# Weighted sums of an adjacency network: narrow matmuls, one row at a time, in place of 512-column blocks and a mask

## The reference

```python
hi = jnp.einsum('bsh,hk->bsk', x, W1[:H])
hj = jnp.einsum('bsh,hk->bsk', x, W1[H:])
h = jax.nn.relu(hi[:, :, None, :] + hj[:, None, :, :] + b1)
y = jnp.einsum('bijk,kl->bijl', h, W2) + b2
y = _layernorm(y, gamma, beta)
out = jnp.einsum('bij,bijh->bih', adj, y)      # the weighted sums
...
x = _layernorm(x + first_layer(x, adj), axis=-1)
x = _layernorm(x + attention_layer(x, adj), axis=-1)
```

## Time and profile before

| | |
|---|---|
| median of 3 runs | 2533.56 us (2532.02 to 2536.31) |
| the profiled execution | 2531.95 us |
| its span, first to last instruction | 2529.9 us |
| TensorE matmuls busy | 2416.6 us (96%) |
| ScalarE busy | 2233.7 us (88%) |
| VectorE busy | 2121.4 us (84%) |
| GpSimd busy | 2024.9 us (80%) |
| TensorE's mean granted clock | 0.986 |

### The profile page before, as it was taken

One profiled execution on the slowest core, in us unless ns is written; L12 is line 12 of the kernel. 1 busy time (PEld: TensorE's weight loads), 2 busy tenths in 40 slices (PEclk: granted clock), 3 DMA queues, 4 the chain that ended last, 5 costly groups with the idle time before them and its releaser, 6 DMA issues.

```text
span 2529.9 us, 182178 instructions
## 1 busy us (share of the span) xinstructions
PE 2416.6 (96%) x73792; PEld 2115.5 (84%) x73792; DVE 2121.4 (84%) x17817; ACT 2233.7 (88%) x3841; POOL 2024.9 (80%) x1227
## 2 busy tenths in 40 slices
PE   8999999999999999999999999999999999999997
PEld 7888888888888888888888888888888888888885
DVE  7888888888888888888888888888888888888887
ACT  7998898888988989888898898988889888898896
POOL 8888887887887878878788787887888877888784
PEclk9999999999999999999999999999999999999999
DMA  0000000000000000000000000000000000000000
GB/s 22 11 10 15 15 10 15 10 15 15 10 15 10 16 15 10 15 11 14 15 10 15 12 14 15 10 16 15 10 15 10 15 15 10 16 14 11 15 8 12
DMA packets 48663, 33.51 MB, mean 13 GB/s; under 512 B 6208, under 2 KB 47808, under 8 KB 47808
## 3 DMA queue, kind: packets, MB, share of 16 engines
q1 hardware_dynamic: 46512, 21.12, 3.0%
q10 hardware_dynamic: 1296, 0.20, 0.0%
HBM read 17.11 MB, written 4.19 MB: 8 GB/s over the span
## 4 chain that ended last, share of the span: by engine, by line
PE 81%; ACT 9%; issue 6%; DVE 4%; POOL 0%; ACTq 0%; DMA 0%; DVEq 0%
PE y_ps L529 60%; PE agg_ps L574 16%; ACT h L288 4%; ACT y L270 3%; DVE squares L515 3%; PE prep_ps L529 2%; PE tail_ps L529 1%; ACT beta_part L328 1%; DVE q L515 1%; PE att_ps L529 1%; ACT ln_v L317 0%; POOL h L259 0%; ACTq L367 0%; DMA beta_rows<-in_L_gnn_beta_dram 0%; ACT rstd L322 0%
## 5 line engine op out<-in xcount | busy, mean ns | idle before, releaser
L259 POOL TENSOR_TENSOR h<-bT,aT 128x1024 f32<-128x1024 f32 x1024 | 1952.7, 1918 | 449.7 <-PE y_ps L529 429.4
L529 PEld LDWEIGHTS y_ps<-w_pair,h 128*32 128x32 f32 x65536 | 1897.4, 111 | 320.0 <-issue 205.5
L529 PE MATMUL y_ps<-w_pair,h 128*32 128x128 f32 x65536 | 2021.6, 275 | 92.4 <-issue 65.5
L515 DVE CUSTOM_DVE_ANT_0 squares<-y_ps,y 128x128 bf16<-128x128 f32 x8192 | 1849.6, 286 | 290.4 <-ACT y L270 283.4
L270 ACT ACTIVATE y<-y_ps 128x508 f32<-128x508 f32 x2048 | 1165.4, 596 | 257.3 <-PE y_ps L529 254.7
L288 ACT ACTIVATE h<-h 128x1024 f32<-128x1024 f32 x1024 | 1084.0, 1059 | 9.5 <-POOL h L259 9.5
L515 DVE DVE_READ_ACCUMULATOR2_ANT q<- 128x1 f32 x8192 | 680.2, 83 | 0.0
L574 PE MATMUL agg_ps<-y,wz 128*32 128x512 f32 x4096 | 568.5, 592 | 0.0
L574 PEld LDWEIGHTS agg_ps<-y,wz 128*32 128x32 f32 x4096 | 158.2, 110 | 2.8 <-issue 2.4
L433 DVE TENSOR_SCALAR tail_ps<-q,bnorm 128x128 f32<-128x128 f32 x64 | 22.7, 354 | 55.9 <-issue 54.5
L451 DVE SCALAR_TENSOR_TENSOR o_sb<-agg_ps,part,o_sb 128x128 f32<-128x128 f32 x192 | 66.6, 347 | 0.2
(11 more groups left out here) (90 smaller groups left out, 734.2 us busy)
## 6 DMA issues: line engine op xcount, KB each, us to landing
x_in<-in_x_dram SPq DMA_DIRECT2D x64, 64.0 KB, 2.3
adj_in<-in_adj_dram SPq DMA_DIRECT2D x64, 64.0 KB, 2.6
x_res<-in_x_dram SPq DMA_DIRECT2D x64, 64.0 KB, 2.1
adj_res<-in_adj_dram SPq DMA_DIRECT2D x64, 64.0 KB, 2.7
out_dram<-x_out SPq DMA_DIRECT2D x64, 64.0 KB, 2.2
w<-in_L_gnn_W_dram ACTq DMA_DIRECT2D x1, 64.0 KB, 2.3
w1a<-in_L_gnn_W_dram SPq DMA_DIRECT2D x1, 64.0 KB, 2.3
w1b<-in_L_gnn_W_dram SPq DMA_DIRECT2D x1, 64.0 KB, 2.3
```

The costliest lines, as they stand in the source:

```text
L259: nc.gpsimd.tensor_tensor(h[:, u % HRING].rearrange("k (r g) s -> k r g s", g=GROUPS), bT[:, p, :].unsqueeze(1).unsqueeze(1).broadcast_to( ...
L515: last = nc.vector.tensor_tensor_reduce(out=squares[:, k % YRING, n, :], in0=y_ps[k % YRING][:, n, :], in1=y[:, p, i, :], scale=1.0, scala ...
L529: last = nc.tensor.matmul(dst[cols], lhsT[:, cols], rhs, start=True, stop=True, tile_position=(0, g * GROUP))
```

## The change

One matmul now handles one row of each group: `wz` has for each group and each of 32 rows a 32-column block with one column that is not zero, and the matmul streams 128 columns. All 32 rows of a group accumulate in the same 128 columns of `agg_ps`, so that partition 32g+r ends with the sum of its own row. The masks, `part` and the semaphores for them are gone; VectorE copies the 128 columns once, at (u, e) = (0, 1). The number of columns that are streamed per slot is the same, the number of matmuls is four times as large. The order on TensorE changes too: the rows stand one or two at a time behind each of the banks k = 8 to 31, in place of 4 rows behind a unit. GpSimd writes `wz` with another pattern of the same number of elements; `wz` has four times the size.

```diff
@@ -54,10 +54,9 @@
 
 
 
-    CHUNK = 4
-    CHUNKS = GROUP // CHUNK
     POOL_WEIGHTS_UNIT, POOL_RESIDUAL_UNIT = 5, 6
-    SUM_AT = {u: c for c, u in enumerate((4, 6, 7, 9, 10, 12, 13, 15))}
+    SUMS_FROM = 8
+    SUMS_STEP = QUARTS - SUMS_FROM
 
     ctx = ExitStack()
     with ctx:
@@ -106,8 +105,7 @@
         q = sb("q", [S, 2, S])
         ln_v = sb("ln_v", [S, S])
         rstd = sb("rstd", [S, S])
-        wz = sb("wz", [S, GROUPS, CHUNKS, GROUP])
-        part = sb("part", [S, CHUNK])
+        wz = sb("wz", [S, GROUPS, GROUP, GROUP])
         o_sb, oT_sb = sb("o_sb", [S, K]), sb("oT_sb", [K, S])
         x1e = sb("x1e", [S, K + 1])
         st1, mv1, ln1, rs1 = sb("st1", [S, 6]), sb("mv1", [S, 2]), sb("ln1", [S, 1]), sb("rs1", [S, 1])
@@ -220,7 +218,7 @@
                 pool.wait_ge(adjT_sb_s, t)
                 if early >= 2:
 
-                    pool.wait_ge(agg_done, (t - 1) * CHUNKS)
+                    pool.wait_ge(agg_done, t - 1)
                 else:
                     pool.wait_ge(s_zero, 1)
                 if early >= 3:
@@ -229,9 +227,9 @@
 
                 flat = wz[:]
                 columns = bass.AP(flat.tensor, flat.offset,
-                                  [list(flat.ap[0]), [CHUNKS * GROUP, GROUPS], [GROUP + CHUNK, CHUNKS], [1, CHUNK]])
-                nc.gpsimd.tensor_tensor(columns, adjT[:, 1 - p, :].rearrange("j (g c s) -> j g c s", g=GROUPS, s=CHUNK),
-                                        rstd[:].rearrange("j (c s g) -> j g c s", g=GROUPS, s=CHUNK), ALU.mult).then_inc(w_ready, 1)
+                                  [list(flat.ap[0]), [GROUP * GROUP, GROUPS], [GROUP + 1, GROUP]])
+                nc.gpsimd.tensor_tensor(columns, adjT[:, 1 - p, :].rearrange("j (g r) -> j g r", g=GROUPS),
+                                        rstd[:].rearrange("j (r g) -> j g r", g=GROUPS), ALU.mult).then_inc(w_ready, 1)
                 nc.gpsimd.tensor_copy(adjS[:, 1 - p, :], adjT[:, 1 - p, :]).then_inc(adjS_ready, 1)
 
             def slot(t, half, p, pairs, prep, gather, tail, early):
@@ -359,7 +357,7 @@
                         for k in range(u * QPU, (u + 1) * QPU):
 
                             if k == 0 and early >= 2:
-                                act.wait_ge(agg_done, (t - 1) * CHUNKS)
+                                act.wait_ge(agg_done, t - 1)
                             if k == 0 and early == 0:
 
                                 act.wait_ge(s_two, 2)
@@ -438,19 +434,13 @@
                             dve.wait_ge(beta_part_ready, t - 2)
                         nc.vector.reduce_sum(adj_sum[:], adj_res[:, p, :], axis=mybir.AxisListType.X).then_inc(adj_sum_ready, 1)
 
-                    if tail and (u, e) == (0, 0):
-
-                        dve.wait_ge(agg_done, (t - 1) * CHUNKS)
+                    if tail and (u, e) == (0, 1):
+
+                        dve.wait_ge(agg_done, t - 1)
                         if early >= 3:
 
                             dve.wait_ge(oT_ps_s, t - 2)
-                        nc.vector.tensor_scalar(o_sb[:], agg_ps[:, 0:K], part[:, 0:1], None, ALU.mult).then_inc(o_part, 1)
-                    if tail and u == 0 and 1 <= e < CHUNK:
-
-                        dve.wait_ge(o_part, (t - 2) * (CHUNK - 1) + e)
-                        nc.vector.scalar_tensor_tensor(out=o_sb[:], in0=agg_ps[:, e * K:(e + 1) * K], scalar=part[:, e:e + 1],
-                                                       in1=o_sb[:], op0=ALU.mult, op1=ALU.add).then_inc(
-                                                           o_stored if e == CHUNK - 1 else o_part, 1)
+                        nc.vector.tensor_copy(o_sb[:], agg_ps[:, 0:K]).then_inc(o_stored, 1)
 
                     if tail and (u, e) == (5, 0):
                         dve.wait_ge(x_beta_ready, t - 1)
@@ -566,14 +556,13 @@
 
             pe.wait_ge(s_ready, 6)
 
-            def weighted_sums(b_parity, chunk):
-
-                y_chunk = y[:, b_parity, chunk * CHUNK * GROUPS:(chunk + 1) * CHUNK * GROUPS, :].rearrange(
-                    "j (r g) m -> j r g m", g=GROUPS)
+            def weighted_sums(b_parity, r):
+
                 for g in range(GROUPS):
-                    last = nc.tensor.matmul(agg_ps[g * GROUP:(g + 1) * GROUP, :], wz[:, g, chunk, :], y_chunk[:, :, g, :],
-                                            start=(chunk == 0), stop=(chunk == CHUNKS - 1), tile_position=(0, g * GROUP))
-                last.then_inc(agg_done, 1)
+                    last = nc.tensor.matmul(agg_ps[g * GROUP:(g + 1) * GROUP, 0:K], wz[:, g, r, :], y[:, b_parity, r * GROUPS + g, :],
+                                            start=(r == 0), stop=(r == GROUP - 1), tile_position=(0, g * GROUP))
+                if r == GROUP - 1:
+                    last.then_inc(agg_done, 1)
 
             def slot(t, half, p, pairs, prep, gather, tail, early):
                 for u in range(UNITS):
@@ -598,23 +587,25 @@
                         pe.wait_ge(eT_ready, t - 1)
                         pe.wait_ge(x1_ready, t - 1)
                         mm(att_ps[:, 0:K + 1], eT[:], x1e[:]).then_inc(att_done, 1)
-                    if pairs:
-
-                        pe.wait_ge(h_ready, t * UNITS + u + 1)
-                        for k in range(u * QPU, (u + 1) * QPU):
+                    for k in range(u * QPU, (u + 1) * QPU):
+                        if pairs:
+                            if k % QPU == 0:
+
+                                pe.wait_ge(h_ready, t * UNITS + u + 1)
                             if not (early == 0 and k < YRING):
 
                                 pe.wait_ge(q_done, t * QUARTS + k - YRING + 1)
                             for n in range(QUART):
                                 last = mm(y_ps[k % YRING][:, n, :], h[:, u % HRING, (k % QPU) * QUART + n, :], w_pair[:])
                             last.then_inc(y_in_psum, 1)
-                    if gather and u in SUM_AT:
-                        if SUM_AT[u] == 0:
-
-                            pe.wait_ge(w_ready, t)
-                            if early >= 2:
-                                pe.wait_ge(o_stored, t - 1)
-                        weighted_sums(1 - p, SUM_AT[u])
+                        if gather and k >= SUMS_FROM:
+                            if k == SUMS_FROM:
+
+                                pe.wait_ge(w_ready, t)
+                                if early >= 2:
+                                    pe.wait_ge(o_stored, t - 1)
+                            for r in range((k - SUMS_FROM) * GROUP // SUMS_STEP, (k + 1 - SUMS_FROM) * GROUP // SUMS_STEP):
+                                weighted_sums(1 - p, r)
 
             run_slots(pe, slot)
 
```

More of the change, by code:

```diff
@@ L132, in gnn_pair_kernel @@
         s_ready = sem("setup_done")
-        s_two, s_zero, s_part = sem("twos_preset"), sem("wz_zeroed"), sem("parts_marked")
+        s_two, s_zero = sem("twos_preset"), sem("wz_zeroed")
         x_loaded, adj_loaded, xres_loaded, stored = (
@@ L140, in gnn_pair_kernel @@
         v_ready, ln_v_ready, rstd_ready, w_ready, adjS_ready = sem("v_ready"), sem("ln_v_ready"), sem("rstd_ready"), sem("w_ready"), sem("adjS_ready")
-        agg_done, o_part, o_stored, oT_ps_s, oT_sb_s, f_ps_s = sem("agg_done"), sem("o_part"), sem("o_stored"), sem("oT_in_psum"), sem("oT_in_sbuf"), sem("f_in_psum")
+        agg_done, o_stored, oT_ps_s, oT_sb_s, f_ps_s = sem("agg_done"), sem("o_stored"), sem("oT_in_psum"), sem("oT_in_sbuf"), sem("f_in_psum")
         x1p_ready, st1_ready, mv1_ready, ln1_ready, rs1_ready = sem("x1p_ready"), sem("st1_ready"), sem("mv1_ready"), sem("ln1_ready"), sem("rs1_ready")
@@ L387, in _ @@
             dve.wait_ge(s_const, 6)
-            nc.vector.reduce_sum(part[:], ident[:].rearrange("p (c s) -> p s c", s=CHUNK), axis=mybir.AxisListType.X).then_inc(s_part, 1)
             nc.vector.tensor_scalar(centre[:], ident[:], -1.0 / K, None, ALU.add).then_inc(s_setup_dve, 1)
@@ L422, in _ @@
             dve.wait_ge(s_ready, 6)
-            dve.wait_ge(s_part, 1)
             def slot(t, half, p, pairs, prep, gather, tail, early):
```

## The result

The changed kernel takes 2853.86 us (median of 4 runs, 2838.57 to 2855.18) against 2532.81 us (2532.02 to 2536.31) for the kernel before on the same chip: a ratio of 1.1247, 95% interval 1.1224 to 1.1270. It is 321 us slower. The prediction had the direction and a tenth of the size: 2567 us, range 2530 to 2585.

A forecast was written before the change was run, and what follows sets the result against it. It took TensorE to be the bound, busy 74.57 of 77.40 us a loop turn. +9.6 + 18.1 + 7.2 - 1.8 = +33.1 us on the profiled 2531.95 gave 2565.1, or 2567 beside the median; range 2530 to 2585.

The forecast's parts named there:

- The narrow form costs 0.15 us a slot: TensorE's sums: 128-column records take 6.99 us a slot against 6.84 before; +9.6 us over 64 slots.
- Their place. Worth 0: TensorE's order: spreading the sums behind 24 banks instead of 8 lumps behind units changes nothing; 0 us.
- The back edge: Loop branch on TensorE: shorter last records hide 0.645 us less of the restart, 28 times; +18.1 us.
- The clock: After loop restarts: longer gaps bring the lower clock in 6 more cases at 1.2 us each; +7.2 us.
- VectorE. So 0: Slot opening: VectorE saves 1.1 us a slot, but ScalarE's chain still holds the ninth bank; 0 us.
- the relief rival: Slot opening: TensorE's waits are VectorE's own, so 33 slots give back 0.45 us each, -14.9; 2526 us; 14%.
- Drain: End of the last slots: one copy replaces the mask steps, 1.2 us earlier, half for the slot before; -1.8 us.
- Weight loads bind: TensorE's sums: each load with new weights needs 38.6 ns; +186 us, some 2750; chance 3%.
- the unseen: Anywhere in the kernel: something the prediction did not foresee, no size named; chance 4%.

The follow-up runs named there:

- before_per_bank: The kernel before with its eight 512-column blocks of sums behind every third bank instead of behind units: 2535.22 us, 1.0001.
- before_badhead: The kernel before, padded so that TensorE's loop body starts at record 204 of a block of 256: 2638.83 us, 1.0407.
- relief: The kernel before with one plain copy for VectorE's four masked steps a slot, leaving out the picking of own columns: 2532.30 us, 0.9994.
- split2: The kernel before with each 512-column matmul of the sums as two of 256 columns, same weights, place and masks: 2629.20 us, 1.0383.

## Why the prediction was wrong

The direction was right, but of the 33 us that made it up only the 9.6 of the stream's rate stand for certain in the 321. Step by step:

- **"The narrow form costs 0.15 us a slot"** is the step that failed. The rate in it was right (27.3 ns a record after the change, as taken). What it left out is that the form also needs 384 more records a slot, 1.5 blocks, and that a slot of the kernel before, 9 blocks in 37.4 us, already had no more than 4.16 us for each. It costs 2.9 us a slot: 183 us measured without the loop, against 9.6.
- **"Their place. Worth 0."** Right: `before_per_bank`, 1.0001.
- **"The back edge", +18.1, and "The clock", +7.2.** The first stop came out near the forecast: the median of 28 is 2.96 us (2.80 to 3.48) for 2.49 before, where 3.1 for 2.5 was forecast. But in `before_badhead`, where the wide block still stands before the branch, the median is 3.19 us, so the lead over the last records can't be called its cause, and the agreement may be luck. The term missed the second stop, which comes from where the branch lands, and the low clock that follows: all 28 restarts have 3.4 us or more at 1.2 GHz behind them, 26 of them 6.8. In the kernel before, the place alone is worth some 97 us.
- **"VectorE. So 0"** and the relief rival at 14%. Right: the sixth bank's wait went, the ninth bank's stayed, and in `relief` the gain went into waits for ScalarE. Its busy time fell by 49.7 us in `relief`, not some 70. In the changed kernel it fell by only 1.7; its squares there count 27 us more in all.
- **"Drain", -1.8.** The copy starts at 2842.39 and the transpose follows at 2842.74, 1.2 us sooner than in the earlier trace rows. As forecast, and lost in the rest.
- **"Weight loads bind"**, at 3%, gave 2750 us, and of the cases given it lies nearest. But its mechanism is wrong: the loads still go out every 27.3 ns between the stops. The truth lay in the 4% of the unseen.

183 us (steady supply) and 97 us (branch target) leave 41 of the 321 us. The two were measured apart from each other, the second in a kernel that is not short of instructions. A loop costs the kernel before 102 us, `before_badhead` 207 with its padding and the changed kernel 239; a kernel short of instructions seems to restart with less in hand, as the 4.23 against 2.55 us suggest. No run isolates that, and it stays open.

What should have warned me was on the page: the instruction queue's packets, set against records of TensorE (633 for 2530 us, one in 4.0 us), and in the weight loads the stop that is put down to "issue", some 2.6 us behind some restarts, of which this is one:

```profile
868.50 2.84 PEld L529 LDWEIGHTS y_ps<-w_pair,h 128*32 128x32 f32 x104 [0.40 <-issue]
```

## What to carry over

Count instructions, not only columns: splitting a matmul is free until the stretch needs blocks of instructions faster than they come, here one of 256 records in some 3.9 us on average, and beyond that the time goes by their number: 40.5 us a slot by that estimate, 40.3 measured without the loop. Divide the span by the instruction queue's packets; where the quotient comes near the shortest that any variant shows, look for idle time called "issue" once a block, and make instructions wider instead of more numerous. The quotient alone doesn't decide: in `split2` it is the shortest of all, and the loss lies at the branches. And before a small effect in a looped kernel is believed, check that it isn't the place of the branch target, or write the loop out.

## What the runs showed of the hardware

- TensorE's instructions come in packets of 16.4 KB, 256 records, and in kernels that wait for them one takes 3.86 to 3.91 us on average, and 3.97 to 4.02 us in the stretches shown. The Trainium skill (Runtime: NRT & Kernel Launch, Instruction fetch mechanics) has the 16 KiB blocks of 256 instructions, and says that crossing into the next is mostly hidden. The kernel before agrees, with 7 us of short stops; the changed one doesn't, with 94 us of them.
- The same section of the Trainium skill says that a taken branch whose target isn't in the current two pages forces a fetch before execution goes on. The trace agrees: 2.2 us and more at each of 28 branches in the kernel before, and in the changed one 1.1 to 2.6 us again after 24 matmul records, its target lying late in its block.
- Moving a loop's first instruction within its block made the kernel before 4% slower (1.0407), with no other edit; a padding of 127 to 179 instructions ahead of the loop took 8 to 12 us of its own, once.
